# Windowed attention with a convolution and an MLP behind it: the five queues written in another order, other PSUM banks, and one more tap of the convolution on VectorE

## What is computed

```python
xw = windows_of_7x7(x)                                  # 2048 windows of 49 tokens, 96 channels
xn = layernorm(xw)
q, k, v = split(xn @ qkv_w.T + qkv_b)                   # 12 heads of 8
attn = softmax(q * SCALE @ k.T + bias)                  # 49x49 for each head and window
seq = x + image_of(attn @ v @ proj_w.T + proj_b)
conv = depthwise_conv_3x3(seq)                          # 9 taps, one weight a channel and tap
seq2 = batchnorm(conv)
out = seq2 + gelu(seq2 @ w1.T + b1) @ w2.T + b2         # 96 -> 384 -> 96
```

## Time and profile before

| | us |
|---|---|
| median of 3 runs | 3465.59 (3450.28 to 3477.62) |
| the profiled execution, device time | 3481.66 |
| its span, first to last instruction | 3479.9 |
| PE busy | 3110.4 |
| DVE busy | 3072.0 |
| ACT busy | 2835.8 |
| POOL busy | 2000.1 |

### The profile page before, as it was taken

How to read it: one execution, slowest core, us unless ns; L and a number is a source line. 1 busy time by engine, 2 the same in 40 slices (tenths; PEclk the granted TensorE clock), 3 DMA queues, 4 the chain that set the end, 5 groups by cost and what they waited for, 6 DMA issues and landing times.

```text
span 3479.9 us, 213611 instructions
## 1 busy us (share of the span) xinstructions
PE 3110.4 (89%) x94988; PEld 2182.9 (63%) x94988; DVE 3072.0 (88%) x4907; ACT 2835.8 (81%) x4883; POOL 2000.1 (57%) x2574
## 2 busy tenths in 40 slices
PE   3889989989989899899899898898998998998986
PEld 2666666666666666666666666666666666666663
DVE  4788989989989899899898898898998988998985
ACT  3888888888878888788888887888887887888875
POOL 2555656556556555556566565565665665655654
PEclk9999999999999999999999999999999999999998
DMA  1333333333333333333333233333333332333321
GB/s 41 93 97 91 100 94 96 99 95 100 95 91 103 94 93 95 93 95 101 93 96 100 87 101 95 93 101 89 99 101 90 98 101 87 101 94 95 101 85 37
DMA packets 269976, 322.92 MB, mean 93 GB/s; under 512 B 55651, under 2 KB 252580, under 8 KB 269062
## 3 DMA queue, kind: packets, MB, share of 16 engines
q1 hardware_dynamic: 236294, 232.12, 23.2%
q0 software_dynamic: 32768, 77.14, 6.4%
HBM read 39.35 MB, written 38.54 MB: 22 GB/s over the span
## 4 chain that ended last, share of the span: by engine, by line
PE 73%; DVE 12%; issue 9%; POOL 4%; ACT 1%; SPq 0%; POOLq 0%; DMA 0%; ACTq 0%; DVEq 0%
PE d_ps L255 22%; PE b_ps L255 16%; PE a_ps L255 11%; PE sm_ps L314 8%; PE st_ps L293 8%; PE o_ps L339 8%; DVE s L738 6%; POOL sl L630 2%; DVE mx L712 2%; DVE y L775 1%; POOL sh L623 1%; DVE ql L746 1%; DVE kl L746 1%; DVE ximg L794 1%; POOL ox L614 0%
## 5 line engine op out<-in xcount | busy, mean ns | idle before, releaser
L738 DVE SCALAR_TENSOR_TENSOR s<-ximg,cols,s 96x392 f32<-96x392 f32 x1792 | 1343.9, 750 | 44.1 <-POOL s L603 7.7
L712 DVE TENSOR_REDUCE mx<-sm_ps 128x12 f16<-128x588 f32 x1024 | 779.0, 761 | 74.5 <-PE sm_ps L314 71.5
L599 POOL TENSOR_TENSOR s<-ximg,cols 96x392 f32<-96x392 f32 x256 | 215.9, 843 | 993.2 <-DVE y L775 992.1
L467 ACT ACTIVATE p<-st_ps 128x588 f32<-128x588 f32 x1024 | 671.3, 656 | 84.0 <-PE st_ps L293 48.8
L314 PEld LDWEIGHTS sm_ps<-k_all,q_all 127*49 127x49 f16 x24576 | 496.5, 104 | 309.3 <-issue 236.4
L255 PE MATMUL d_ps<-g,w_s 128*64 128x392 f32 x3072 | 675.1, 507 | 3.0 <-ACT g L518 2.1
L293 PE MATMUL st_ps<-q_all,k_all 128*49 128x49 f16 x24576 | 541.1, 186 | 70.8 <-issue 66.3
L614 POOL DMA_DIRECT2D ox<-o_sb x1024 | 580.8, 570 | 36.0 <-ACT o_sb L492 16.2
L293 PEld LDWEIGHTS st_ps<-q_all,k_all 128*49 128x49 f16 x24576 | 480.7, 104 | 190.3 <-issue 105.1
L314 PE MATMUL sm_ps<-k_all,q_all 127*49 127x49 f16 x24576 | 527.8, 186 | 57.7 <-issue 54.1
L339 PE MATMUL o_ps<-p,v 128*32 128x49 f32 x24576 | 398.8, 210 | 35.1 <-issue 33.0
(11 more groups left out here) (114 smaller groups left out, 6156.5 us busy)
## 6 DMA issues: line engine op xcount, KB each, us to landing
ox<-o_sb POOLq DMA_DIRECT2D x1024, 73.5 KB, 2.3
k_all<-kh SPq DMA_DIRECT2D x512, 96.0 KB
q_all<-qh SPq DMA_DIRECT2D x512, 96.0 KB
x_sb<-in_x SPq DMA_DIRECT2D x256, 147.0 KB, 3.1
out<-y SPq DMA_DIRECT2D x256, 147.0 KB
k_all<-kl SPq DMA_DIRECT2D x256, 96.0 KB
q_all<-ql SPq DMA_DIRECT2D x256, 96.0 KB
q_all<-mxt SPq DMA_DIRECT2D x256, 12.0 KB, 2.0
```

The costliest lines, as they stand in the source:

```text
L467: af(p32[:, p, :, :].rearrange("p (b h) n -> p b h n", b=2), st_ps[:, :, 0:HALF].rearrange("p b (h n) -> p b h n", n=TOK), ACT.Exp).then_i ...
L712: v.tensor_reduce(mx[:, c % 2, :, p].rearrange("p (b h) -> p b h", b=2), sm_ps[:, :, 0:HALF].rearrange("p b (h n) -> p b h n", n=TOK), AX. ...
L738: v.scalar_tensor_tensor(acc, image_rows(c, k // 3, k % 3), cw_c[:, k:k + 1], acc, ALU.mult, ALU.add)\
```

## The change

Nothing is computed otherwise. The lists of calls in the five queues are written in another order and with other leads, the PSUM banks that hold the long products are dealt out anew, the waits follow from that, and tap 1 goes from POOL to DVE, which takes away POOL's second product and its sum. `wide` is now called `halves`; it is the same function.

```diff
-STEPS = CHUNKS + 8
+STEPS = CHUNKS + 11
...
-                wide(b_ps[0:128, 0:CT], avg[:, :], sq[:, :]).then_inc(var_done, 1)
+                halves(a_ps[0:128, 0:CT], avg[:, :], sq[:, :]).then_inc(var_done, 1)
...
-                free(pe, (sum_done, c-5), (v32_done, c-2), (ql_done, c-1))
-                wide_three(a_ps[0:128, 0:CT], wq_h[:, 0:128], wq_l[:, 0:128], xh[:, c % 2, :, 0:TOK], xl[:, c % 2, :, 0:TOK]).then_inc(q_done, 1)
+                free(pe, (kl_done, c+0), (g_done[1], c-7), (v32_done, c-2), (ql_done, c-1))
+                halves_three(b_ps[0:128, 0:CT], wq_h[:, 0:128], wq_l[:, 0:128], xh[:, c % 2, :, 0:TOK], xl[:, c % 2, :, 0:TOK]).then_inc(q_done, 1)
...
-            hidden_ps = {0: b_ps, 1: d_ps, 2: b_ps}
+            hidden_ps = {0: d_ps, 1: b_ps, 2: a_ps}
...
-                acc, one = (t.rearrange("c (r q) -> c r q", q=SIDE) for t in (s2[0:C, c % 2, :], part[:, :]))
-                weight = lambda k: cw_c[:, k:k + 1].unsqueeze(2).broadcast_to([C, WS, SIDE])
                 wait(pool, sum_done, c)
                 wait(pool, y_done, c - 2)
-                tt(acc, image_rows(c, 0, 0), weight(0), ALU.mult).then_inc(tap_done[0], 1)
-                tt(one, image_rows(c, 0, 1), weight(1), ALU.mult).then_inc(part_done, 1)
-                wait(pool, tap_done[0], c)
-                pool.wait_ge(part_done, 1 * c + 1)
-                tt(acc, acc, one, ALU.add).then_inc(tap_done[1], 1)
+                tt(s2[0:C, c % 2, :].rearrange("c (r q) -> c r q", q=SIDE), image_rows(c, 0, 0),
+                   cw_c[:, 0:1].unsqueeze(2).broadcast_to([C, WS, SIDE]), ALU.mult).then_inc(tap_done[0], 1)
...
-                maxima(s - 2, 0)
-                block_out(s - 8)
-                key_low(s - 1)
...
+                maxima(s - 2, 1)
+                normalise(s - 5)
+                maxima(s - 2, 2)
```

More of the change, by code:

```diff
@@ L84, in block_program @@
         sh, sl = sb("sh", [C, CT], F16), sb("sl", [C, CT], F16)
-        part = sb("part", [C, CT])
         g = sb("g", [128, NB, CT])
@@ L250, in _, with halves @@
             mm = nc.tensor.matmul
-            def wide(o, w, m, start=True, stop=True):
+            def halves(o, w, m, start=True, stop=True):
                 for h in range(2):
@@ L416, in second @@
                 wait(pe, g_done[k], c)
-                if k == 1:
-                    free(pe, (g_done[1], c+0), (xn_done, c+7), (y_done, c-1))
-                wide(d_ps[0:128, 0:CT], w2_s[:, k, :], g[:, k, :], start=k == 1, stop=k == 0).then_inc(s_done[k], 1)
+                if k == 2:
+                    free(pe, (g_done[2], c+0), (sum_done, c+2), (lnv_done, c+7), (y_done, c-1))
+                halves(a_ps[0:128, 0:CT], w2_s[:, k, :], g[:, k, :], start=k == 2, stop=k == 1).then_inc(s_done[k], 1)
             for s in range(STEPS):
+                maxima_rows(s - 3)
+                exp_scores(s - 4, 3)
+                values_times_p(s - 4, 1)
+                keys(s - 1)
+                centred(s)
+                max_scores(s - 2, 0)
+                second(s - 8, 2)
+                queries(s - 1)
+                second(s - 8, 0)
+                second(s - 8, 1)
+                exp_scores(s - 3, 0)
+                values_times_p(s - 4, 3)
                 values_times_p(s - 4, 2)
-                centred(s)
+                max_scores(s - 2, 1)
+                exp_scores(s - 3, 1)
+                variance(s)
                 max_scores(s - 2, 2)
-                exp_scores(s - 3, 1)
                 values(s - 2)
-                variance(s)
                 exp_scores(s - 3, 2)
-                values_times_p(s - 3, 0)
-                values_times_p(s - 3, 1)
+                projection(s - 5)
                 max_scores(s - 2, 3)
                 hidden(s - 7, 0)
-                projection(s - 5)
+                values_times_p(s - 3, 0)
                 hidden(s - 7, 1)
-                maxima_rows(s - 2)
-                exp_scores(s - 3, 3)
                 hidden(s - 7, 2)
-                second(s - 7, 1)
-                keys(s)
-                second(s - 7, 2)
-                max_scores(s - 1, 0)
-                second(s - 7, 0)
-                queries(s)
-                max_scores(s - 1, 1)
-                exp_scores(s - 2, 0)
-                values_times_p(s - 3, 3)
         @block.scalar
@@ L532, in log_variance @@
                 wait(act, var_done, c)
[L533 removed]
+                af(rstd[:, :], a_ps[0:C, 0:CT], ACT.Ln, bias=eps_c).then_inc(lnv_done, 1)
             def root(c):
@@ L550, in _ @@
             for s in range(STEPS):
+                act.preload_act_table_set("natural_log_exp_and_others")
+                exp(s - 4, 3)
+                square(s)
+                outputs(s - 4, 0)
+                log_sums(s - 5)
+                query_high(s - 1)
+                inverses(s - 5)
                 exp(s - 3, 0)
-                log_sums(s - 5)
-                inverses(s - 5)
-                square(s)
                 outputs(s - 4, 1)
@@ L772, in block_out @@
                     return
-                wait(dve, s_done[0], c)
+                wait(dve, s_done[1], c)
                 dve.wait_ge(stored[c % 2], (c // 2 + 1) * 16)
-                v.scalar_tensor_tensor(y[0:C, c % 2, :], d_ps[0:C, 0:CT], b2_c, s2[0:C, c % 2, :], ALU.add, ALU.add)\
+                v.scalar_tensor_tensor(y[0:C, c % 2, :], a_ps[0:C, 0:CT], b2_c, s2[0:C, c % 2, :], ALU.add, ALU.add)\
                  .then_inc(y_done, 1)
@@ L799, in _ @@
             for s in range(STEPS):
[L800 to L802 removed]
                 maxima(s - 2, 1)
[L804 to L806 removed]
+                normalise(s - 5)
                 maxima(s - 2, 2)
[L808 to L814 removed]
+                input_normal(s)
+                values_out(s - 2)
+                image_sum(s - 5)
+                maxima(s - 2, 3)
+                tap(s - 6, 1)
+                maxima_out(s - 2)
+                tap(s - 6, 2)
                 tap(s - 6, 3)
                 tap(s - 6, 4)
+                key_low(s)
                 tap(s - 6, 5)
                 tap(s - 6, 6)
+                maxima(s - 1, 0)
+                tap(s - 6, 7)
+                block_out(s - 7)
+                query_low(s)
+                tap(s - 6, 8)
 def kernel(x, L0_conv_ln_g, L0_conv_ln_b, L0_conv_qkv_w, L0_conv_qkv_b, L0_conv_proj_w, L0_conv_proj_b,
```

77 lines of the change are left out of this document (31 added, 46 removed).

## The result

The changed kernel takes 3571.57 us (median of 4 runs, 3569.0 to 3584.49), the kernel before 3466.3 us in the same comparison: a ratio of 1.0306, interval 1.0283 to 1.0328. It is slower by 3.1%; I had forecast 3370 us and faster.

A forecast was written before the change was run, and what follows sets the result against it. A loop through several engines (12.30 us) plus 0.79 of PE pauses bounds the kernel; the new loop of 12.39 plus 0.3 gives 12.7 a step, 255 x 12.7 + 142.8 = 3381.3, scaled to the median 3370 us; range 3240 to 3490.

The forecast's parts named there:

- the room for PE's pauses: On PE: products fill about 11.1 us of a step, so the new loop leaves over 1 us where pauses cost nothing.
- a loop of 12.39: New loop through DVE and POOL, from xl's end through taps, y, tap 8, sh, sl to xl: 12.39 us a step.
- tight passages: On PE: kl's start to y, 2.72 us against DVE's 2.87, and the transposed maxima behind the hidden layer.
- tap 8's hold: On DVE: tap 8 held by POOL's tap 0, ending 2.02 us after y's start instead of 1.62, 0.40 held.
- the 0.3 for the pauses: On PE: what is left of the old 0.79 us of pauses a step, with 0 and 0.79 as ends.
- The pauses' nature: On PE: pauses are instructions that come late, 252 a packet and three packets a step.
- Rival 2: PE's pauses stay: 13.18 us a step, 3490 us on the median, within 1% of before; chance 0.18.
- Rival 3: DVE becomes the bound, slower, with tap 1's 0.66 on top: 13.75 us a step, 3634 on the median; chance 0.12.
- The old loop: Loop of 12.30 us through DVE, POOL and PE: cut by the change, 10.5 in the new order, no longer counts.
- Tap 1 is held: On DVE: tap 1 waits under POOL's xl and lets the next instruction start 0.34 us after xl's end.
- The longer lead: STEPS + 3 adds steps in which only SP's store runs; nothing is charged.
- DVE above PE: Sign of a right forecast: DVE's busy time in the changed kernel lies above PE's.

The follow-up runs named there:

- a_pool_tap: The changed kernel with taps 0 and 1 back on POOL as before, DVE making taps 2 to 8: 3645.3 us, 1.0538 of the kernel before.
- a_run178: The changed kernel with 14 more waits a step between the run's five short groups, a packet end at 434: 4140.78 us, 1.1966 of the kernel before.
- a_split: The changed kernel with centred moved between the two value products, cutting the run in two, and its square later on ACT: 3615.18 us, 1.0431 of the kernel before.
- a_spread: The changed kernel with 14 more waits a step in seven pairs behind long products, 175 ahead of the loop: 3423.84 us, 0.9864 of the kernel before.
- b_spread: The kernel before with 14 more waits a step in seven pairs behind long products, 144 ahead of the loop: 3396.17 us, 0.979 of it.
- a_one: The changed kernel with each long product as one matmul of 128 weight columns instead of two of 64: 3490.39 us, 1.006 of the kernel before.

## Why the prediction was wrong

**The step that failed** is the one on the room for PE's pauses: "PE's products fill about 11.1 of a step [...], so a loop of 12.39 leaves it over 1 us, where a pause costs nothing." The 11.1 is too little: in the chain of the changed kernel PE's own work from value products to value products is 11.94 us, so an undisturbed step of 12.35 leaves it 0.4 and not over 1 (PE's busy time in a short step of the old order, 12.03 of 12.30, had pointed that way). And a sum over a whole step says nothing of where the room lies, since a queue that runs in order has it only where its loop has it. The loop from the third scores through hidden layer, keys, queries and second layer to y, ql, tap 8 and the maxima holds all but the run of short groups. From 1611.15 to 1621.33 are 10.18 us, 9.37 without the 0.81 of pause; with the 2.76 from y to PE it makes 12.13, 0.22 under the undisturbed step, which the loop through DVE and POOL sets. Every pause outside the run comes through but for this, and one in the run has 0.24 besides. I had looked for tight passages one at a time and named two, and closed neither into a loop with tap 8 in it, though I had tap 8's hold in the sum.

**The term that was mis-sized** is the 0.3 for the pauses, whose upper end I had at 0.79. It measured 13.45 - 12.35 = 1.10. The upper end took for granted that no order could let more through than the old one. The new one lets nearly all of the 0.96 through, and the run of five groups, which I placed "where PE has room", holds the longest pauses on average, 1.1 to 1.6 us, with the lower clock behind many of them; what is over 0.96 is no more than the clock can cost, 0.16.

**The pauses' nature** I had right, and could have used it: 252 instructions a packet and three packets a step were in the prediction, but I spread the pauses evenly instead of asking where the packets end. The Trainium skill, "Runtime: NRT & Kernel Launch", section on instruction fetch mechanics, has blocks of 256 and the cost of crossing one mostly hidden. The runs bear out the 256 (272 of 272 pauses at one place) and not the hiding: 0.94 us of 13.09 a step. By that rule, with the pauses put down to something that the new order leaves as it is, I would have ended at 3490, also too low.

**The rivals.** Rival 2, pauses stay, is the nearest in its mechanism: 13.18 forecast, 13.45 measured. Rival 3 had the sign, and a step of 13.75, by another cause: it wanted DVE kept for more than 1.8 us a step beside its work. DVE was indeed 2.15 us a step beside its 11.30 (13.45 - 11.30), but 1.3 of that it stood idle (3107.8 over 256 is 12.14 busy), the undisturbed step of 12.35 shows that DVE isn't the bound at 13.75, and a_pool_tap says that the tap on DVE gains. No rival of mine had the pauses cost more than before, and that was the case that came.

**Right** were these. The old loop is gone, and the undisturbed step is 12.35 for 12.39. Tap 8 is held under POOL's tap 0: 1.01 at 1608.15, with an end 0.42 us after POOL's, as under the sum. POOL's timeline:

```profile
1601.00 0.93 POOL L587 TENSOR_TENSOR xl<-xn,xh 96x392 f16<-96x392 f32 x1
1607.90 0.84 POOL L595 TENSOR_TENSOR s<-ximg,cols 96x392 f32<-96x392 f32 x1 [5.98 <-DVE y L768]
```

The Trainium skill, "SBUF — State Buffer", section on who interferes with whom, has a VectorE instruction with two SBUF inputs contend with a GpSimd instruction that reads SBUF: the trace agrees. Tap 1 is held only when xl runs: 1.02 at 1601.33, under this xl, but 0.61 at 1615.08, when the next xl (1613.59 to 1614.49) was over. The longer lead is free. **Wrong** was DVE above PE: the holds that went and the ones that came nearly cancel the extra tap, 3107.8 for 3072.0.

**Open** stays why a packet is asked for late when an end lies in the run. Rests of 0.1 to 0.2 us between its groups didn't bring the request forward (a_run178), and cutting the run once doesn't change it (a_split, which also lengthened the undisturbed step). Nor did I settle how the 1.10 splits between the pauses (0.96 in all), the clock (at most 0.16) and taps and maxima thrown out of their places. Why the old order lets less of its pauses through, 0.79 of 0.94, I haven't traced in its steps. And the 0.8% between a_spread and b_spread may be the orders or the choice of places.

## What to carry to other kernels

When a kernel spends its time in short instructions, count them: find where PE's unexplained pauses stand modulo 256, make the loop's count a multiple of it by waits behind long instructions, and choose the places of the ends; here that gave 2.1% on the order before, and the same steps with the ends in bad places took 11.7% longer than in good ones (3822.82 over 3423.84). Before calling time on an engine spare, follow every wait on that engine back to itself through the others, and ask how long the loop is with each held instruction in it. And compare two orders only at the same places of the packet ends, since an order that moves them mixes both effects.

## What the runs showed of the hardware

- A packet of PE's instructions ends every 256. Fetching one takes about 1.1 us, PE goes on 1.4 us after it has landed, and it is asked for from about 0 to 3.5 us after the end before (medians), by where the ends lie. Pauses of up to 2.22 us in the kernel before, and 2.57 in a_run178, come from it.
- A fulfilled wait on PE isn't free. In a row ahead of the loop an instruction of two such waits takes 0.107 us (first xn at 61.8 with 144 of them and at 50.6 with 40: 11.2 us for 104), behind short matmuls 0.08 (1.16 for fourteen, where two of my expectations reckoned 0.051 each), behind a long product less of it shows (0.2 and 0.5 for fourteen).
- A group of 24 short matmuls takes 0.43 us behind a product of 128 weight columns (a_one), 0.32 behind one of 64 (the changed kernel).
- After a pause of 1.96 us the granted clock was 0.64 for the next 4.7 us.
